# Attention scores in 24 units instead of 28, with a head's third and first query tile in one bank and masks on all 128 rows behind dense blocks

## What is computed

```python
scores = jnp.einsum('bhqd,bhkd->bhqk', q, k) / jnp.sqrt(jnp.float32(hd))
causal = jnp.tril(jnp.ones((s, s), dtype=bool))
scores = jnp.where(causal, scores, -jnp.inf)
weights = jax.nn.softmax(scores, axis=-1)
attn = jnp.einsum('bhqk,bhkd->bhqd', weights, v)
```

## Time and profile before

| | |
|---|---|
| Median of 3 runs | 1868.26 us (1855.72 to 1869.14) |
| Span of the profiled execution | 1852.8 us |
| PE, PEld busy | 1700.5 us (92%), 1360.0 us (73%) |
| DVE busy | 1437.1 us (78%) |
| ACT, POOL busy | 976.7 us (53%), 1056.0 us (57%) |
| mean granted PE clock | 0.959 |

### The profile page before, as it was taken

One profiled execution on the slowest core, in us unless ns is written; L12 is line 12 of the kernel. 1 busy time (PEld: TensorE's weight loads), 2 busy tenths in 40 slices (PEclk: granted clock), 3 DMA queues, 4 the chain that ended last, 5 costly groups with the idle time before them and its releaser, 6 DMA issues. The chain is left out here.

```text
span 1852.8 us, 49530 instructions
## 1 busy us (share of the span) xinstructions
PE 1700.5 (92%) x14718; PEld 1360.0 (73%) x14719; DVE 1437.1 (78%) x3985; ACT 976.7 (53%) x2048; POOL 1056.0 (57%) x1446
## 2 busy tenths in 40 slices
PE   5899999999999999999999998589999986988883
PEld 4677777777777777777777775368888876877773
DVE  4589899999999899899999996378888971455554
ACT  1166666666676666666666765333444422544441
POOL 4045555555555655655555556446777770567666
PEclk8899999999999999999999999679999997999996
DMA  2555556556556555555565453223333356999996
GB/s 76 80 132 152 141 128 158 142 119 166 141 135 144 147 147 138 135 154 142 123 162 141 123 147 99 109 74 105 126 120 120 122 155 169 286 327 326 323 331 220
DMA packets 226548, 291.13 MB, mean 157 GB/s; under 512 B 57142, under 2 KB 188954, under 8 KB 226458
## 3 DMA queue, kind: packets, MB, share of 16 engines
q1 hardware_dynamic: 190042, 186.14, 40.3%
q0 software_dynamic: 18048, 49.31, 8.2%
q10 hardware_dynamic: 18368, 54.64, 7.7%
HBM read 83.25 MB, written 129.69 MB: 115 GB/s over the span
## 5 line engine op out<-in xcount | busy, mean ns | idle before, releaser
L752 ACT ACTIVATE probs<-bank 128x376 f32<-128x376 f32 (+2 forms) x896 | 440.7, 529 | 272.9 <-PE bank L621 261.0
L843 DVE TENSOR_REDUCE neg_max<-bank 120x1 f32<-120x376 f32 (+2 forms) x896 | 507.0, 587 | 53.7 <-PE bank L587 49.7
L587 PE MATMUL bank<-k_rows,q_rows 64*128 64x128 f32 (+2 forms) x1536 | 403.7, 345 | 3.1 <-ACT probs L752 2.4
L621 PE MATMUL bank<-q_rows,k_rows 64*120 64x120 f32 (+2 forms) x1536 | 369.9, 336 | 3.9 <-ACT probs L752 3.6
L982 POOL TENSOR_SCALAR_AFFINE_SELECT probs<-probs 128x512 f32<-128x512 f32 (+1 forms) x384 | 232.4, 631 | 209.5 <-ACT probs L752 209.3
L604 PE MATMUL bank<-causal,own_row 56*120 56x56 bf16 (+4 forms) x1792 | 300.9, 248 | 8.7 <-DMA k_rows<-k_flat_hi 3.5
L587 PEld LDWEIGHTS bank<-k_rows,q_rows 64*128 64x128 f32 (+1 forms) x1536 | 246.2, 186 | 6.7 <-ACT probs L752 4.6
L2205 POOL DMA_INDIRECT y_got<-y_sorted,p_route x188 | 182.4, 970 | 119.7 <-issue 117.6
L621 PEld LDWEIGHTS bank<-q_rows,k_rows 64*128 64x128 f32 (+1 forms) x1536 | 229.8, 183 | 8.7 <-ACT probs L752 5.8
L604 PEld LDWEIGHTS bank<-causal,own_row 64*128 64x128 bf16 (+2 forms) x1792 | 153.4, 115 | 110.3 <-DVE neg_max L843 39.9
L1847 POOL DMA_INDIRECT x_sorted<-r_normed,route x188 | 184.3, 981 | 83.6 <-issue 59.0
(11 more groups left out here) (235 smaller groups left out, 4148.8 us busy)
## 6 DMA issues: line engine op xcount, KB each, us to landing
x_sorted<-zeros ACTq DMA_DIRECT2D x32, 816.0 KB, 3.8
y_sorted<-zeros ACTq DMA_DIRECT2D x32, 816.0 KB, 4.3
x_rows<-x_sorted SPq DMA_DIRECT2D x51, 512.0 KB, 6.4
y_sorted<-p_y_rows SPq DMA_DIRECT2D x51, 512.0 KB, 6.4
q_rows<-q_flat_hi SPq DMA_DIRECT2D x256, 94.0 KB
k_rows<-k_flat_hi SPq DMA_DIRECT2D x248, 94.0 KB
q_rows<-q_flat_lo SPq DMA_DIRECT2D x128, 94.0 KB
out_dram<-base SPq DMA_DIRECT2D x47, 256.0 KB, 5.0
```

Source lines behind the costliest of these rows:

```text
L587: last = eng.matmul(ps[0:T[t], m * w:(m + 1) * w], q[rows, slot, t * P:t * P + T[t]], k[rows, slot, 0:w], start=False, stop=(m == len(head ...
L621: last = eng.matmul(ps[0:T[t], m * w:(m + 1) * w], k[64 * c:64 * c + 64, slot, t * P:t * P + T[t]], q[64 * c:64 * c + 64, slot, t * P:S], ...
L752: eng.activation(probs[g % 2][0:T[t], first:first + len(heads), OFF[t]:OFF[t] + w], bank_exp[n % 2][0:T[t], 0:len(heads) * w].rearrange("k ...
L843: eng.tensor_reduce(dst, src, AX.X, ALU.max, negate=True).then_inc(max_taken, 1)
```

## The change

A group has six units instead of seven: units 0 and 1 are the second query tile of two heads each, units 2 to 5 the third and the first tile of one head, side by side in one bank of 512 columns. For maxima all units are 512 columns wide and 128 rows high (rows past the 376th token hold padding), and the maximum of a third-tile row comes as three parts that `turn_maxima` joins with a new small reduction. Exps become 24 of 496 columns. In the 13 units that stand behind a dense block the mask is one product on all 128 rows (`own_whole`, `causal_whole`); the 11 others keep two on their 64 rows. Dense blocks are joined and moved: hid0 and hid1 at n=1, values at 5 and 23, conv0 and conv1 at 7, normed_T at 9, q0 and q1 at 13, k0 and k1 at 15, out at 18 and 20, products with values at 3, 11, 16, 21. On DVE take_lo moves one unit behind its block, to n=8 (conv), 10 (normed_T), 14 (q) and 16 (k), each after that unit's maxima. POOL's masks go to tile order 1, 0, 2, of which 0 and 2 need all six units. SP issues load_x behind max_rows(1). Not shown: the exp's new operands, the clearing's second place (n=19), wider k rows with zeros behind the 376th token, and the old halves of some edits.

```diff
-    GROUPS, UNITS = 4, 7
+    GROUPS, UNITS = 4, 6
     CUT = [S - P * t for t in range(NT)]
-    OFF = [0, CUT[0], CUT[0] + CUT[1]]
+    OFF = [0, CUT[0] + CUT[2], CUT[0]]
...
+                eng.memset(causal_whole[:, :, :], 0.0).then_inc(zeroed, 1)
+                eng.memset(own_whole[:, :], 0.0).then_inc(zeroed, 1)
+                eng.wait_ge(zeroed, 5)
...
+                eng.affine_select(out=own_whole[:, :], in_=own_whole[:, :], compare_op=ALU.not_equal, fill=1.0,
...
+                eng.affine_select(out=causal_whole[:, :, :], in_=causal_whole[:, :, :], compare_op=ALU.is_ge,
...
+                eng.wait_ge(idents, 11)
...
-                return (["hid0", "hid1"] * front + ["val0"] * maxima
+                return (["hid0", "hid1"] * front + ["val0"] * maxima + ["conv0", "conv1"] * mix
                         + ["nT0", "nT1", "q0", "q1", "k0", "k1"] * front
-                        + ["out0", "out1"] * finish + ["conv0", "conv1"] * mix + ["val1"] * maxima)
+                        + ["out0", "out1"] * finish + ["val1"] * maxima)
...
+        VALUES_AT = (3, 11, 16, 21)
+        WHOLE_MASK = (0, 2, 4, 6, 8, 10, 12, 14, 16, 17, 19, 21, 22)
...
+                        eng.wait_ge(max_taken, st.at(1, GROUPS * UNITS, n - 2))
...
+                    rows = slice(64 * (g % 2), 64 * (g % 2) + 64)
+                    if u < PAIRS:
+                        slot, t, at = 4 * (g // 2) + 2 * u + m, 1, 2 * P * m
+                    else:
+                        slot, t, at = 4 * (g // 2) + u - PAIRS, (2, 0)[m], NT * P * m
+                    keys = min(S, (t + 1) * P)
+                    last = eng.matmul(ps[:, at:at + keys], q[rows, slot, t * P:(t + 1) * P], k[rows, slot, 0:keys],
+                                      start=False, stop=(m == 1), skip_group_check=True)
...
+                    if u < PAIRS:
+                        blocks = ps[:, 0:4 * P].rearrange("q (m w) -> q m w", m=2)[:, :, P:2 * P]
+                    else:
+                        blocks = ps[:, 2 * P:4 * P].rearrange("q (m w) -> q m w", m=2)
+                    if g * UNITS + u in WHOLE_MASK:
+
+                        eng.matmul(blocks, own_whole[:, :], causal_whole[:, :, :],
+                                   start=True, stop=False, skip_group_check=True)
+                        return
...
+                        eng.matmul(blocks[:, :, 64 * h:P], own_row[rows, h, :], causal[rows, h, 0:2, 64 * h:P],
                                    start=(h == 1), stop=False, skip_group_check=True)
...
-                        if n in (1, 2) and st.front:
-                            hid_rows(st, n - 1)
-                        if u == 4:
+                        if n == 1 and st.front:
+                            hid_rows(st, 0)
+                            hid_rows(st, 1)
+                        if n in VALUES_AT:
...
+                                if group < 0 and st.finish:
                                     products_with_values(st, 3, -1, t)
-                                if g > 0 and st.attend:
-                                    products_with_values(st, g - 1, 0, t)
...
+                                    products_with_values(st, group, 0, t)
+                        if n == 5 and st.maxima:
                             values(st, 0)
+                        if n == 7 and st.mix:
+                            conv(st, 0)
+                            conv(st, 1)
...
-                        if n in (13, 15) and st.front:
-                            query_key(st, "q", (13, 15).index(n), w_q)
-                        if n == 17 and st.front:
+                        if n == 13 and st.front:
+                            query_key(st, "q", 0, w_q)
+                            query_key(st, "q", 1, w_q)
...
-                        if n in (20, 22) and st.finish:
-                            out_rows_(st, (20, 22).index(n))
-                        if n in (24, 27) and st.mix:
...
-                        if n == 27 and st.maxima:
+                        if n in (18, 20) and st.finish:
+                            out_rows_(st, (18, 20).index(n))
+                        if n == 23 and st.maxima:
...
                             exps(st, g, u)
-                        if n == 14 and st.attend:
+                        if n == 10 and st.attend:
                             clear_pages(st, x_sorted)
...
-                        if n == 5 and st.finish:
+                        if n == 4 and st.finish:
...
                             normalise(st)
-                        if st.front and n in (9, 10):
-                            take_hi(st, f"nT{n - 9}", nT[st.b % 2][0][:, n - 9, :])
...
+                        if st.mix and n == 7:
+                            for j in range(2):
+                                take_hi(st, f"conv{j}", mixed[0][:, j, :])
+                        if st.front and n == 9:
+                            for j in range(2):
+                                take_hi(st, f"nT{j}", nT[st.b % 2][0][:, j, :])
+                        if n in (12, 17, 22) and st.attend:
+                            keep(st, (12, 17, 22).index(n), 0)
...
-                        if st.front and n in (13, 15):
-                            j = (13, 15).index(n)
-                            take_hi(st, f"q{j}", q_flat[0][:, j, :], bias=bias_q[:, j:j + 1])
-                        if st.front and n == 17:
+                            for j in range(2):
+                                take_hi(st, f"q{j}", q_flat[0][:, j, :], bias=bias_q[:, j:j + 1])
+                        if st.front and n == 15:
                             for j in range(2):
                                 take_hi(st, f"k{j}", k_flat[0][:, j, :], bias=bias_k[:, j:j + 1])
...
-                HALF_1_AT = {10: (0, 1), 12: (2,), 14: (3,), 16: (4,)}
-                HALF_0_AT = {21: (0,), 23: (1, 2), 25: (3,), 26: (4,)}
-                HI = ["nT0", "nT1", "q0", "q1", "k0", "k1", "conv0", "conv1"]
+                HALF_1_AT = {9: (0,), 11: (1,), 12: (2, 3), 13: (4,)}
+                HALF_0_AT = {19: (0,), 21: (1,), 22: (2, 3), 23: (4,)}
+                HI = ["conv0", "conv1", "nT0", "nT1", "q0", "q1", "k0", "k1"]
...
+                    half, e = g // 2, g % 2
+                    if u < PAIRS:
+                        src = max_bank(n)[:, 0:4 * P].rearrange("q (m w) -> q m w", m=2)
+                        dst = neg_max[:, half, 4 * e + 2 * u:4 * e + 2 * u + 2, 4]
+                    else:
+                        src = max_bank(n)[:, 0:4 * P].rearrange("q (c w) -> q c w", c=4)
+                        dst = neg_max[:, half, 4 * e + u - PAIRS, 0:4]
...
+                    whole = neg_max[:, half, :, 3:6].rearrange("q (c m) t -> q t c m", c=2)
...
+                    eng.tensor_reduce(neg_max[:, half, :, 5], neg_max[:, half, :, 0:3], AX.X, ALU.min).then_inc(max_joined, 1)
+                    eng.wait_ge(max_joined, done)
...
-                        if n == 19 and st.maxima:
+                        if n == 16 and st.maxima:
...
-                        if st.front and n == 2:
+                        if n == 0 and st.attend:
+                            turn_maxima(st, 1, 0)
+                        if st.front and n == 1:
                             hid_out(st, 0)
                             hid_out(st, 1)
+                        if st.front and n == 2:
                             norm_stats(st)
...
-                            turn_maxima(st, 1, 0)
-                        if st.maxima and n == 7:
...
+                        if st.mix and n == 8:
+                            for j in range(2):
+                                take_lo(st, f"conv{j}", mixed[1][:, j, :], mixed[0][:, j, :])
+                        if st.front and n == 10:
+                            for j in range(2):
+                                take_lo(st, f"nT{j}", nT[st.b % 2][1][:, j, :], nT[st.b % 2][0][:, j, :])
...
-                        if st.front and n in (13, 15):
-                            j = (13, 15).index(n)
-                            take_lo(st, f"q{j}", q_flat[1][:, j, :], q_flat[0][:, j, :], bias=bias_q[:, j:j + 1])
-                        if st.front and n == 17:
+                        if st.front and n == 14:
+                            for j in range(2):
+                                take_lo(st, f"q{j}", q_flat[1][:, j, :], q_flat[0][:, j, :], bias=bias_q[:, j:j + 1])
+                        if st.front and n == 16:
                             for j in range(2):
                                 take_lo(st, f"k{j}", k_flat[1][:, j, :], k_flat[0][:, j, :], bias=bias_k[:, j:j + 1])
+                        if st.finish and n in (18, 20):
+                            out_sum(st, (18, 20).index(n))
                         if st.attend and n in HALF_0_AT:
                             for piece in HALF_0_AT[n]:
                                 gather_sums(st, 0, 0, piece)
...
-                        if st.maxima and n == 27:
```

(45 more changed lines are left out.)

93 lines of the change are left out of this document (32 added, 61 removed).

## The result

The changed kernel takes 1937.05 us, the median of 4 runs (1935.45 to 1944.75), against 1868.7 for the kernel before beside it: a ratio of 1.0407 (95% interval 1.036 to 1.0453). The forecast was 1907 us, at most 1928. The sign and the four new waits came as forecast; the size did not, and 1937 us lies outside the range.

The account below looks back on a forecast made before the run. TensorE sets the step before; after, its order with stalls and the DMA loop, in parallel, give 35.4 us instead of 34.06. 29 x 1.35 + 0.5, about 39 us, on the median 1868.26 gives 1907 us; range 1862 to 1928.

Parts of the forecast that it names:

- normed_T on mixed_lo: At n=9 TensorE waits for conv0's bank, which VectorE reads behind the maxima of unit 8: stall 0.8 us.
- k0 on q_flat_lo: At n=15 TensorE waits for q0's bank, which VectorE reads behind the maxima of unit 14: 0.9 to 1.1 us.
- values on GpSimd's masks: Group 2's products, moved to n=21, wait for three masks that GpSimd does after join(0): stall 1.0 us.
- The first half of the loop: From a step's first score to q1's reading, on the loop through the DMA queue: 21.9 us.
- Parallel roads: TensorE's step with stalls (35.5 us) and the loop through the DMA queue (34.9 to 35.5) run in parallel, not adding.
- the loop's last term: Landing, from the last copy's issue to the waiting score: 1.2 us, read from a tail step.
- may hit fewer copies: 34.9: ScalarE's clearing transfer, moved to n=19, may slow fewer q copies, shortening the DMA loop from 35.5 to 34.9 us.
- TensorE's own step: TensorE's step without stalls: 34.06 - 1.5 - 0.6 - 0.4 + 1.2, about 32.7 us (32.1 to 33.0).
- I count 29: 28 steps with all stages and two partial ones, counted as 29, each 1.35 us longer.
- the carry-over: The old kernel's median lies 15.5 us above its profiled span; the same distance was added to the forecast span.
- Worse: Rival: VectorE adds stalls or TensorE's clock falls in gaps; from 36.0 us a step, 1925 us and above; chance 0.08.
- 35.0 to 35.8: The main forecast for one attention step in us, giving 1895 to 1920 us by itself; chance 0.58.

Follow-up runs that it names:

- e3: Changed kernel with the products with values of group 2, and the whole mask behind them, one unit later (22 instead of 21): 1939.17 us, ratio 1.0422.
- e1: Changed kernel with ScalarE issuing the transfer that clears y_sorted behind exp 1 instead of exp 19: 1929.67 us, ratio 1.0361.
- e5: Changed kernel with every hand-over pulled apart (clearing behind exp 1, q subtractions and normed_T moved, keep of group 1 earlier): 1876.93 us, ratio 1.0059.
- e6: e5 with eight reciprocals of 94 columns cut to one column each, less work for VectorE: one run, 1860.76 us.
- e13: Changed kernel with q's subtractions ahead of maxima 14 and group 2's products behind unit 22, clearing left behind exp 19: 1919.94 us, ratio 1.0295.
- e4: Changed kernel with both edits of e13 and the clearing transfer behind exp 1: 1879.99 us, ratio 1.0085.
- e9: Changed kernel with conv back behind k, hand-overs pulled apart and all masks in halves: 1930.12 us, ratio 1.0351.
- e14: e5 with all masks in halves, and four copies of the maxima issued by ScalarE behind exp 20 instead of by SyncE: 1860.9 us, ratio 0.9978.

## Why the prediction was right, and where it fell short

**Right.** *The waits.* normed_T on mixed_lo 0.86 (0.8 forecast), k0 on q_flat_lo 0.89 (0.9 to 1.1), values on GpSimd's masks 0.98 (1.0), the first scores on the maxima's DMA: all four names, and the three sizes that were given. TensorE's busy time near 32 us a step (32.53), VectorE's 31.91 (31.3). *The first half of the loop*: 21.72 from first score to q1's reading, 21.9 forecast. *Parallel roads*: e3 shows that they don't add.

**The terms that were mis-sized.** The mechanism held; the sizes did not. The step of the prediction that failed is the loop's last term, 1.2 us of landing, which measured 1.9 to 2.0; behind it come the number of steps and the opening. (a) *The landing behind the last copy.* The sum took 13.6 from q1's reading to the next first score, 12.4 of issues and 1.2 of landing, and said of the clearing transfer that moved to unit 19 it "may hit fewer copies: 34.9". It hits the last ones. The 12.4 held by luck: it had the transfer's 0.65 in it, at the head, and at the tail the transfer adds 0.6 to the issues again. To the landing it adds 0.7 to 0.8: 1.88 in the step shown, 1.99 in the median, and not 1.2. The 1.2 had come from a tail step, where no such transfer runs beside the copies. That makes 36.0 and not 35.5: 1.93 over 34.06 where 1.35 was taken, times 29 steps 17 us.

(b) *TensorE's own step*, 32.1 and not 32.7. 0.23 of that are the whole masks, 0.13 behind products with values instead of 0.20 among them; the rest is spread over blocks that no run prices. With the three waits behind unit 0 it makes 35.0, so it was the shorter road and did not decide. Dense to half rows costs 0.10 more at the block's end than dense to whole rows, and products with values (32-column tiles) to either costs the same: this fits an array that is emptied at each change of mode. The Trainium skill, TensorEngine Tiling, Tiling Modes (Key Properties), says that a change of mode drains TensorE; the trace agrees in kind, and the extra price behind products with values is 0.08, half of the 0.15 taken.

(c) *The number of steps and the set-up.* "I count 29" and 0.5 for set-up (29 x 1.35 + 0.5 is 39.7, put down as 39). Up to the first product of the stage behind attention (1195.2 before, 1267.2 after) the traces differ by 72.0: 3.1 up to the first q product (37.9 to 41.0), 11.8 in the four steps behind it (137.1 long before, 148.9 after), 50.6 in the next 26 (1.95 each), 6.5 in the rest. The partial steps at both ends grow as well, and the first four steps by 3 each, at a clock of 0.85 in 40 to 140 us (0.92 before). That is 16 us more than 29 x 1.93.

(d) *The span and the median.* The traces differ by 83 us, the medians by 68. 11 of the 83 lie in stages that the change does not touch (657.6 us from that product to the end before, 668.6 after; 661.7 to 673.0 in the experiments). The profiled execution of the kernel before was its fastest, and the prediction carried its distance to the median over, 15.5 us; the changed kernel's median lies 1.2 above its span. In sum the span was forecast 44 us too short, 17 by (a), 16 by (c) and 11 by (d), and the carry-over 14 too long: 1937 for 1907.

The rival that came nearest, *Worse* from 36.0 us on, named VectorE and the clock; the clock stayed at 1.00 in the steady steps and VectorE's lateness showed only once the copies were out of the way (e1, e5, e6). The chance of 0.58 for 35.0 to 35.8 was too high for a sum whose last term came from a tail step.

## What to carry to other kernels

When a loop of several engines sets the period, follow it round once with its own rows, and look at every transfer that another queue runs beside its last copies: one clearing transfer among them cost 1.3 us a step against the same transfer issued elsewhere. A wait beside that loop is free, so undo edits in pairs (e13 against e4) before pricing one by what it gives back alone (e1: 0.3). And a block of work that seems misplaced may be the cover for a chain on other engines: before moving it, ask who is idle while it runs.

## What the runs showed of the hardware

**Two queues, the same DMA engines.** From 418 to 424 us of the changed kernel (queue: packets, MB, share of 16 engines):

```profile
q10 hardware_dynamic: 272, 0.84, 41.9%
q1 hardware_dynamic: 544, 0.42, 32.5%
```

q10 is ScalarE's clearing, q1 SyncE's copies. The Trainium skill, DMA: Bandwidth & Descriptors, Issuing engines are not separate DMA queues, says that transfers issued by SP and ACT run on the same 16 engines and interleave there. The trace agrees: a copy of 6 KB lands 0.7 us later beside 816 KB of another queue (e13 against e4). SP's four issues take longer too, 3.40 for 2.81; what they share with ScalarE's transfer while they are issued, no run tells.

**A gap costs twice.** Waits of up to 1 us each, spread over a step, left the clock at 1.00 throughout. TensorE busy for 0.58 of 2 us (e9) was followed by 3.3 us at 0.50.

**Issuing costs the issuer.** Four copies took 2.90 us of ScalarE (e14), during which its next exp stood still, as they take 2.81 of SP.
